# Slot mixer: when GpSimd adds the output's bias to the residual rows

## What is computed

```
x = x + tanh(g_ffn[3]) * slot_mixer(layernorm(x))

slot_mixer(x):                     # 64 slots, top 8 of them for each token
    alpha = top8_softmax((gelu([x, mean slot] @ w1 + b1) @ w2 + b2) / (|tau| + 0.1))
    si    = (alpha^T x) / sum(alpha)
    r, z  = sigmoid(si @ Wih + bih + S @ Whh + bhh), its first two thirds
    n     = tanh(i_n + r * h_n)
    S_new = (1 - z) * n + z * S                    # a GRU step of the slots
    y     = layernorm(S_new + attention(S_new))    # q, k, v of S_new; 64 x 64 scores
    return (alpha @ (y @ wvp + bvp)) @ wo + bo
```

## Time and profile before

| what | value |
|---|---|
| median of 3 runs | 1800.82 us |
| lowest, highest | 1793.05, 1805.83 us |
| the profiled execution | 1798.77 us |
| its span in the profile | 1796.9 us |
| its mean granted clock of TensorE | 0.95 of full |

### The profile page before, as it was taken

How to read it: one execution, slowest core, us unless ns; L and a number is a source line. 1 busy time by engine, 2 the same in 40 slices (tenths; PEclk the granted TensorE clock), 3 DMA queues, 4 the chain that set the end, 5 groups by cost and what they waited for, 6 DMA issues and landing times.

```text
span 1796.9 us, 31011 instructions
## 1 busy us (share of the span) xinstructions
PE 1619.2 (90%) x9150; PEld 1153.7 (64%) x9150; DVE 981.3 (55%) x3200; ACT 624.8 (35%) x1772; POOL 333.5 (19%) x465
## 2 busy tenths in 40 slices
PE   6898899859999999999999999799998998887787
PEld 2555555659999866666666667567776446665555
DVE  4778787542222244444444435645555666884764
ACT  3555555412323233333333333133332004552232
POOL 4555555320000130000000000100000122333000
PEclk8999999869999989999999989899998999998887
DMA  4000005248999610000000000100000001310000
GB/s 109 15 18 20 20 19 146 65 138 298 321 327 319 232 41 13 7 12 12 12 12 6 1 4 16 31 26 19 19 25 1 27 25 35 91 56 1 1 19 19
DMA packets 86297, 115.80 MB, mean 64 GB/s; under 512 B 16610, under 2 KB 77762, under 8 KB 81090
## 3 DMA queue, kind: packets, MB, share of 16 engines
q1 hardware_dynamic: 82722, 110.43, 19.1%
q0 software_dynamic: 2432, 4.34, 0.8%
q10 hardware_dynamic: 1056, 0.01, 0.0%
HBM read 104.51 MB, written 6.95 MB: 62 GB/s over the span
## 4 chain that ended last, share of the span: by engine, by line
PE 73%; issue 9%; DVE 7%; ACT 4%; DMA 2%; POOL 2%; ACTq 1%; SPq 0%; DVEq 0%; POOLq 0%
PE bank L2293 14%; PE bank L2406 8%; PE bank L2589 7%; PE bank L2379 5%; PE bank L2682 5%; PE bank L2352 5%; PE bank L2390 4%; PE bank L2436 4%; PE bank L2603 3%; PE bank L2344 3%; PE bank L2635 3%; PE bank L2651 3%; PE bank L2754 2%; DMA work<-in_F_b1c 2%; DVE work L1542 1%
## 5 line engine op out<-in xcount | busy, mean ns | idle before, releaser
L1052 ACT ACTIVATE work<-bank,work 100x361 f32<-100x361 f32 (+1 forms) x272 | 158.9, 591 | 253.5 <-DVE work L1542 231.6
L1551 DVE COPY work<-bank 128x300 f32<-128x300 f32 (+1 forms) x272 | 123.2, 490 | 175.6 <-PE bank L2390 174.9
L2406 PEld LDWEIGHTS bank<-work 128*100 128x100 f32 x1760 | 185.4, 171 | 45.5 <-issue 31.4
L2406 PE MATMUL bank<-work 128*100 128x64 f32 (+1 forms) x1760 | 188.2, 258 | 4.2 <-DVE work L1551 4.2
L2589 PE MATMUL bank<-work 128*128 128x128 f32 x1216 | 144.4, 277 | 3.7 <-DMA work<-in_F_b1c 3.7
L1905 DVE SCALAR_TENSOR_TENSOR work<-bank,work 128x128 f32<-128x128 f32 x160 | 56.1, 351 | 163.8 <-PE bank L2589 151.6
L2589 PEld LDWEIGHTS bank<-work 128*128 128x128 f32 x1216 | 142.0, 193 | 5.3 <-issue 3.5
L1542 DVE TENSOR_REDUCE work<-bank 100x1 f32<-100x361 f32 x208 | 101.8, 528 | 70.9 <-PE bank L2379 65.7
L823 POOL TENSOR_TENSOR work<-work,neg_half 100x1 f32<-100x1 f32 x96 | 52.5, 547 | 391.8 <-DVE work L1498 390.1
L2379 PE MATMUL bank<-work 64*100 64x361 f32 (+1 forms) x512 | 119.0, 542 | 1.1 <-ACT work L1037 0.6
L2293 PE MATMUL bank<-L_WkvT,work 96*128 96x512 f32 x192 | 98.2, 637 | 15.8 <-ACT work L1013 14.9
(11 more groups left out here) (306 smaller groups left out, 2907.9 us busy)
## 6 DMA issues: line engine op xcount, KB each, us to landing
work<-in_F_w SPq DMA_DIRECT2D x58, 1024.0 KB, 5.5
work<-in_ctxT SPq DMA_DIRECT2D x64, 135.4 KB, 2.1
work<-in_ctx SPq DMA_DIRECT2D x32, 192.0 KB, 2.5
work<-in_F_b SPq DMA_DIRECT2D x20, 128.0 KB, 5.8
work<-sorted_x SPq DMA_DIRECT2D x20, 128.0 KB, 2.5
sorted_y<-work SPq DMA_DIRECT2D x20, 128.0 KB, 5.3
work<-in_ctx SPq DMA_DIRECT2D x32, 78.8 KB, 2.4
F_weight<-in_F_w SPq DMA_DIRECT2D x2, 1024.0 KB
```

The lines of the kernel that those rows point to most:

```text
L1052: nc.scalar.activation(pr[:, 0:NK], S_bank[k][0:T, 0:NK], ACT.Exp, bias=nmax[k][0:T, :], accum_out=rsum[j][0:T, h:h + 1]).then_inc(s.exped ...
L1551: nc.vector.tensor_copy(PT[k][:, 0:CH, :], PT_bank[k][:, 0:CH * T].rearrange("p (c t) -> p c t", c=CH)).then_inc(s.probs_copied.sem, 1)
L2406: ins = nc.tensor.matmul(to, PT[k][:, c, :], values, start=(c == 0), stop=(c == CH - 1))
```

## The change

GpSimd's additions of the bias wait for one semaphore more: `s_turned` must have reached 1, which it does when TensorE has turned couple 0's new slots in the first round. Nothing else is changed.

```diff
@@ -936,6 +936,7 @@
                 mixture_tokens(3, B - 1)
 
                 pool.wait_ge(s.bo_scaled, 1)
+                pool.wait_ge(s.s_turned, 1)
                 for u in range(B // 2):
                     nc.gpsimd.tensor_tensor(X[0:T, 2 * u:2 * u + 2, :], X[0:T, 2 * u:2 * u + 2, :],
                                             Sbo[0:T, :].rearrange("p (o d) -> p o d", o=1).broadcast_to([T, 2, D]), ALU.add
```

## The result

The changed kernel takes 1808.56 us in the median of 19 runs, the kernel before 1799.76 us in the median of 19. One of the changed kernel's runs took 2738.36 us at a mean granted clock of 0.551, and the ratio goes by the other 18 (median 1807.09 us, clock 0.95). The ratio is 1.0045, with a 95% interval of 1.0031 to 1.0060: 8.1 us slower (5.6 to 10.8). The forecast was 7.9. All lines behind the added one have moved on by one (L940 is L941, L2036 is L2037, L2106 to L2120 are L2107 to L2121, L2749 is L2750, L2790 is L2791, L2754 is L2755).

A forecast was written before the change was run, and what follows sets the result against it. In the edited stretch DVE's chain of 15 instructions was taken to bound the kernel. The first add's 0.85 us and seven more at 1.00 made some 7.9 us, added to the 1800.82 us median: 1808.7 us, range 1800 to 1815.

The forecast's parts named there:

- Nothing to gain: Ahead of L2044: removing the adds' overlap frees L2036's 0.78 us, all inside 2.90 us of idle time; gain 0.
- The adds start at the transpose of couple 0, on the DVE chain of 15 instructions: First round, L2106 to L2120: adds start near 1688.5, 0.28 us before L2106, with 15 SBUF-only DVE instructions ahead.
- They take turns, every 1.42 us: First round's DVE chain: add and DVE instruction alternate every 1.42 us; eight held, 0.85 plus seven at 1.00, 7.85 us.
- The rule of one pair: L2036 beside adds 4 and 5: one data pass each in turn, 1.69 us per pair, 1.42 for 256-element DVE passes.
- Nothing hides it: After the last L2120: last transpose, qkv, attention and all that follows come later by the same 7.9 us.
- TensorE's clock at no extra price: TensorE's products after the idle stretch: clock already low there, 1.83 us paid now, so added cost 0.
- No loss: Rival at DVE's handovers: DVE's next request beats the waiting add; time 1800.8 or 1800.0 us; chance 0.13.
- Whole adds: Rival in the first round's DVE chain: each add blocks DVE for all its 1.26 us; +9.8, 1810.6 us; chance 0.13.
- The clock for longer: Rival on TensorE: two more couples' products run at 1.2 GHz; 7.9 + 3.7 = 11.6, 1812.4 us; chance 0.11.
- The number: Whole kernel: median 1800.82 + 7.9 = 1808.7 us, range 1800 to 1815; forecast case's chance 0.63.

The follow-up runs named there:

- The memsets: Kernel before, adds early, plus 12 GpSimd memsets of 100x512 into unused weights once the first slots are turned; ratio 0.9998 (0.9982 to 1.0014).
- copies: Kernel before, adds early, plus 8 GpSimd copies of 100x512 from SBUF to SBUF once the first slots are turned; ratio 1.0019 (1.0000 to 1.0037).

## Why the prediction was right, point by point

- *Nothing to gain.* Right. L2036's stall lay in idle time; without it the idle time ahead of L2045 grew from 2.90 to 3.69 us, and the kernel without adds had the time of the kernel before.
- *The adds start at the transpose of couple 0, on the DVE chain of 15 instructions.* Right. They began at 1687.18, 0.21 us ahead of the first held instruction (L2107 at 1687.39); I had said 0.28.
- *They take turns, every 1.42 us.* Right: 1.40 to 1.42 measured. The rule of one pair, L2036 against adds 4 and 5, was enough, with 0.27 us taken off for the shorter pass. Eight held at 1.34 to 1.49 us in the timeline (the chain, which counts from the end of the instruction before, has 1.27 to 1.42); the adds in 11.11 us, where I had said 11.2. The first instruction lost 0.92 us (0.85 forecast), the sum was 7.78 (7.85). L2036's own 0.69 us, borrowed from a line that reads PSUM, is 0.68 without adds beside it. The last L2121 ended at 1701.54 and not near 1703, because the stretches ahead of the round were 1.38 us shorter in this profile.
- *Nothing hides it.* Right: from the last slots_new to the end the two profiles differ by 0.4 us in 102.
- *TensorE's clock at no extra price.* Right for the change. The experiments show that it was not a matter of course: with the chain 1.38 us shorter, TensorE's products behind the second round took 1.3 us more.
- *No loss.* Falls with the first held instruction. *Whole adds* (9.8 us) falls with the period of 1.41 instead of 1.26 + 0.42 = 1.68. *The clock for longer* falls with couple 1's 1.09 us.
- *The number.* The size was worked out and came true in the stretch, 7.78 for 7.85. That the time, 1808.7 forecast, met the median of 1808.56 so closely is luck: the median of the 18 runs behind the ratio is 1807.09, and the ratio leaves 5.6 to 10.8 us open.

The Trainium skill, page "SBUF — State Buffer", section "Who interferes with whom", says that a DVE instruction with two SBUF inputs contends with a GpSimd instruction that reads SBUF and not with one that only writes. The memsets bear that out (0.42 to 0.43 us under them), as the adds and copies do the first half. That the loser blocks for the whole instruction, as the prediction cites from there, is nearly so: the pair's period is 0.2 us longer than GpSimd's own, less than DVE's 0.42, so the ends of two instructions overlap.

## What to carry to other kernels

A GpSimd instruction that reads SBUF beside a chain of DVE instructions with two SBUF inputs is not free work: each one that meets such an instruction puts its own period (1.23 us for an add of 100x512, from its start to the next one's where none is held) plus 0.2 us less DVE's 0.42 us onto the chain. That is some 1.0 us for the add and 0.33 for a copy of that size. A multiply and add with constants like L2106 belongs to such a chain too. Place such work of GpSimd's where DVE reads PSUM or waits, which a list of DVE's operands shows, and not merely where GpSimd is idle. And where the runs scatter by several us, a stretch that the edit touches, cut at the same instructions in two profiles, tells 0.2 us apart.

## What I had not expected of the hardware

- L2106, one SBUF input of 512 elements in 0.42 us, is held by GpSimd's writes too, and holds them (the prediction did not have this; I allowed for it only ahead of the run with the memsets): 0.52 us instead of 0.42, and the memset beside it 0.80 instead of 0.52. With adds or copies beside it, it is held as the two-input ones are (1.34 and 0.60 us for the first).
- TensorE's return to full speed is not tied to the moment at which its work resumes. In the kernel before couple 1's q and k took 1.12 us in the second round, in the one with the shorter DVE chain 1.97, 3.9 us after the first product of that stage in both. With the longer values a chain shortened by 1.38 us so gave back nearly all of it, 1.28 us. Why the clock rose later there, no run shows.
